# Narrow fp32 products of an attention kernel split into fp32r pairs, with the first image's start reordered and the last store halved

## Reference

```python
# x: (16, 64, 64, 256), W_qkv: (256, 768), W_out: (256, 256), b_out: (256)
g = group_norm(x, 32 groups)                # mean and variance over pixels and 8 channels
q, k, v = split(g @ W_qkv, 3)               # per image: n = 4096 pixels, c = 256 channels
k = softmax(k, over the 4096 pixels)
context = einsum('bdn,ben->bde', k, v)      # 256 x 256 per image
out = einsum('bde,bdn->ben', context, q)
return x + out @ W_out + b_out
```

## Time and profile before

| | |
|---|---|
| median of 3 runs | 1215.73 us (1215.03 to 1215.77) |
| profiled execution | 1216.79 us, of which the span of its instructions 1215.1 us |
| TensorE busy (PE) | 1190.2 us, 98% |
| VectorE (DVE), ScalarE (ACT), GpSimdE (POOL) busy | 840.8, 839.5, 621.4 us |
| HBM traffic | 218 GB/s over the span |

### The profile page before, as it was taken

The page is one execution under the profiler, slowest core; times in us unless marked ns, Lnnn a source line. Parts: engine busy times, 40 slices in busy tenths (PEclk is TensorE's granted clock), DMA queues, the critical chain, the costliest instruction groups (busy, mean ns, idle before and its releaser), DMA issues.

```text
span 1215.1 us, 21446 instructions
## 1 busy us (share of the span) xinstructions
PE 1190.2 (98%) x8460; PEld 1116.2 (92%) x8460; DVE 840.8 (69%) x1582; ACT 839.5 (69%) x1140; POOL 621.4 (51%) x288
## 2 busy tenths in 40 slices
...
GB/s 318 149 166 295 232 234 204 193 273 208 276 200 200 264 172 296 223 206 234 163 302 229 224 220 185 283 208 259 203 206 261 181 281 230 190 254 123 189 84 160
DMA packets 107061, 266.71 MB, mean 219 GB/s; under 512 B 10192, under 2 KB 10192, under 8 KB 106960
## 3 DMA queue, kind: packets, MB, share of 16 engines
...
HBM read 198.18 MB, written 67.11 MB: 218 GB/s over the span
## 4 chain that ended last, share of the span: by engine, by line
PE 96%; DVE 1%; ACT 1%; DMA 1%; issue 0%; SPq 0%; DVEq 0%; ACTq 0%
PE ps_k L385 29%; PE ps_e L548 19%; PE ps_e L557 10%; PE ps_g L476 5%; PE ps_e L464 5%; PE ps_e L476 5%; PE ps_e L466 5%; PE ps_g L464 5%; PE ps_g L466 5%; PE ps_g L495 1%; PE ps_g L512 1%; PE ps_g L526 1%; PE ps_g L518 1%; DVE bn L819 1%; PE ps_g L501 1%; DMA xs<-in_xt_dram 1%
## 5 line engine op out<-in xcount | busy, mean ns | idle before, releaser
L327 POOL TENSOR_TENSOR xt_lo<-xt_raw,xt_hi 128x1024 fp32r<-128x1024 f32 x128 | 307.4, 2404 | 435.3 <-ACT xt_hi L655 309.6
L333 POOL TENSOR_TENSOR x_lo<-x_raw,x_hi 128x1024 fp32r<-128x1024 f32 x128 | 280.2, 2206 | 67.7 <-ACT x_hi L660 58.2
L869 DVE TENSOR_TENSOR mx<-ps_k,mx 128x256 f32<-128x256 f32 x480 | 203.3, 423 | 96.3 <-ACT e_raw L664 74.9
L712 ACT ACTIVATE o_stage<-ps_e,bias 128x512 f32<-128x512 f32 x253 | 170.5, 688 | 114.8 <-PE ps_e L557 114.8
L385 PE MATMUL ps_k<-wk_hi,xt_hi 128*128 128x256 f32 x1024 | 207.3, 285 | 0.0
L385 PE MATMUL ps_k<-wk_lo,xt_hi 128*128 128x256 f32 x1024 | 205.3, 283 | 0.0
L664 ACT ACTIVATE e_raw<-ps_k 128x512 f32<-128x512 f32 x256 | 141.2, 594 | 88.4 <-PE ps_k L385 88.4
L826 DVE BATCH_NORM_STATS2 bn<-xs 128x6 f32<-128x512 f32 x240 | 154.2, 685 | 38.5 <-DMA xs<-in_xt_dram 37.5
L672 ACT ACTIVATE e_hi<-e_raw 128x1024 fp32r<-128x1024 f32 x128 | 135.0, 1055 | 59.1 <-DVE e_raw L894 29.8
L385 PEld LDWEIGHTS ps_k<-wk_hi,xt_hi 128*128 128x128 f32 x1024 | 163.5, 190 | 7.0
L385 PE MATMUL ps_k<-wk_hi,xt_lo 128*128 128x256 f32 x1024 | 158.2, 283 | 0.0
...
## 6 DMA issues: line engine op xcount, KB each, us to landing
xt_raw<-in_xt_dram SPq DMA_DIRECT2D x128, 512.0 KB, 4.3
x_raw<-in_xn_dram SPq DMA_DIRECT2D x128, 512.0 KB, 3.5
out_dram<-o_stage SPq DMA_DIRECT2D x128, 512.0 KB, 4.5
xs<-in_xt_dram SPq DMA_DIRECT2D x240, 256.0 KB, 5.0
w_setup<-in_w_dram SPq DMA_DIRECT2D x2, 256.0 KB, 9.9
wk<-in_w_dram SPq DMA_DIRECT2D x1, 256.0 KB, 10.3
wq_t<-in_w_dram SPq DMA_DIRECT2D x1, 256.0 KB, 11.3
...
```

The costliest lines, as they stand in the source:

```text
L327: nc.gpsimd.tensor_tensor(xt_lo[:, s], xt_raw[:, s], xt_hi[:, s].bitcast(F32), ALU.subtract).then_inc(xt_lo_ready, 1)
L333: nc.gpsimd.tensor_tensor(x_lo[:, s], x_raw[:, s], x_hi[:, s, :, 0:C].bitcast(F32), ALU.subtract).then_inc(x_lo_ready, 1)
L712: nc.scalar.activation(o_stage[:, u % O_SLOTS, h, :], src, ACT.Identity, bias=bias[:, h:h + 1]).then_inc(o_ready, 1)
L869: nc.vector.tensor_tensor(mx[:], tile, mx[:], ALU.max).then_inc(max_done, 1)
```

## The change

The maxima, the variances (from image 1 on) and the negated means are each split on VectorE into an fp32r part and its fp32r rest (new small tiles `m_blk_hi`, `m_blk_lo`, `var_hi`, `var_lo`, `nm_parts`), and the products with them take fp32r operands: 2 matmuls for a plain one in `spread_max` and `stats_var`, and in `bias_sum` the two parts of `m` as weights with both parts of the mean as two columns. `bias_sum` goes from behind the first `emit_high` to behind the second `emit_high` and the first `emit_low`; the bias is added up in two steps. The identity and `grp` are converted to fp32r once, by ScalarE. In image 0 the maxima of block 0 lie in `ps_e`, so that the first gather waits only for `wvo_lo_ready`; half of `wv @ wo` goes behind keys 3; `turn_max` goes behind keys 4 and `spread_max` behind keys 5; shift 3 goes behind the maxima of keys 7, and ScalarE's exponentials 1 and 2 go behind the last `keys_out`. The last chunk is stored in two halves, each when its half is ready.

The diff, cut to its core:

```diff
+        def max_psum(b, blk):
+
+            return ps_e if b == 0 and blk == 0 else (ps_g0, ps_k[:, 0])[blk]
...
+            def store_last():
+                for h in range(CB):
+                    sp.wait_ge(o_ready, B * (CB * NCH) - CB + h + 1)
+                    sp.dma_start(out_chunks[bass.ds((B - 1) * NCH + EMIT_ORDER[NCH - 1], 1), :, h, :].rearrange("a p n -> (a p) n"),
+                                 o_stage[:, (NCH - 1) % O_SLOTS, h, :]).then_inc(last_stored, 16)
...
+                    if b == B - 1 and u == NCH - 1:
+                        store_last()
+                    elif not late(b, u, CB - 1):
                         store(b, u)
...
             def spread_max(b, blk):
 
-                to = (ps_g0, ps_k[:, 0])[blk]
-                pe.wait_ge(m_blk_ready, b * 2 + (blk + 1))
-                for d in range(CB):
-                    last = nc.tensor.matmul(to[:, 1, d * P:(d + 1) * P],
-                                            m_blk[:, blk, d:d + 1].broadcast_to([P, P]), ident,
-                                            start=(d == 0), stop=True, skip_group_check=True)
+                to = max_psum(b, blk)
+                for part, ready in ((m_blk_hi, m_blk_hi_ready), (m_blk_lo, m_blk_lo_ready)):
+                    pe.wait_ge(ready, b * 2 + (blk + 1))
+                    for d in range(CB):
+                        last = nc.tensor.matmul(to[:, 1, d * P:(d + 1) * P],
+                                                part[:, blk, d:d + 1].broadcast_to([P, P]), ident_r,
+                                                start=(part is m_blk_hi and d == 0), stop=(part is m_blk_lo),
+                                                skip_group_check=True)
                 last.then_inc(bc_ps, 1)
...
             def stats_var(b):
-                pe.wait_ge(var2_ready, b + 1)
-                nc.tensor.matmul(stats_psum(b, 1), grp[:], var2[:], start=True, stop=True).then_inc(var_ps, 1)
+                if b == 0:
+                    pe.wait_ge(var2_ready, 1)
+                    nc.tensor.matmul(stats_psum(0, 1), grp_r[:].bitcast(F32), var2[:], start=True,
+                                     stop=True).then_inc(var_ps, 1)
+                    return
+                for part, ready in ((var_hi, var_hi_ready), (var_lo, var_lo_ready)):
+                    pe.wait_ge(ready, b)
+                    last = nc.tensor.matmul(stats_psum(b, 1), grp_r[:], part[:], start=(part is var_hi),
+                                            stop=(part is var_lo))
+                last.then_inc(var_ps, 1)
...
             def gather_high(b, j):
                 pe.wait_ge(e_hi_ready, b * NCH + (j + 1))
-                if j == 0:
+                if b == 0 and j == 0:
+                    pe.wait_ge(wvo_lo_ready, 1)
+                elif j == (HALF if b == 0 else 0):
                     pe.wait_ge(sub_done, b * NCH + HALF)
...
-            def bias_sum(b, parity):
-                pe.wait_ge(m_full_ready, b + 1)
+            def bias_sum(b):
+                pe.wait_ge(nm_parts_ready, b + 1)
+                _, hi, lo = combined(b)
                 for h in range(CB):
-                    for c in range(CB):
-                        last = nc.tensor.matmul(ps_g0[:, 0, h:h + 1], m_full[:, c, h * P:(h + 1) * P],
-                                                neg_mean[:, parity, c:c + 1], start=(h == 0 and c == 0),
-                                                stop=(c == CB - 1), skip_group_check=True)
+                    for part in (hi, lo):
+                        for c in range(CB):
+                            last = nc.tensor.matmul(ps_g0[:, 0, 2 * h:2 * h + 2], part[:, c, h * P:(h + 1) * P],
+                                                    nm_parts[:, c, :], start=(h == 0 and part is hi and c == 0),
+                                                    stop=(part is lo and c == CB - 1), skip_group_check=True)
                 last.then_inc(bias_ps, 1)
...
+            pe.wait_ge(grp_r_ready, 1)
             stats_mean(0)
             stats_var(0)
...
-            for c in range(CB):
+
+            def values_out(c):
                 for e in range(CB):
                     last = nc.tensor.matmul(ps_g0[:, c, 0:C], wv_t[:, e, c * P:(c + 1) * P], wo[:, e, :],
                                             start=(e == 0), stop=(e == CB - 1))
-            last.then_inc(setup_ps, 1)
+                last.then_inc(setup_ps, 1)
+
+            values_out(0)
             first_keys_high()
             keys_low(0, 0, 0, 0, TILES)
             for j in range(1, HALF):
                 keys(0, 0, j)
+            values_out(1)
             pe.wait_ge(wq_loaded, 16)
             for d in range(CB):
-                last = nc.tensor.matmul(ps_e[:, 0, 0:C], one_col[:].broadcast_to([P, P]), wq_t[:, d, :],
+                last = nc.tensor.matmul(ps_e[:, 1, 0:C], one_col[:].broadcast_to([P, P]), wq_t[:, d, :],
                                         start=(d == 0), stop=(d == CB - 1))
             last.then_inc(setup_ps, 1)
-            pe.wait_ge(wvo_lo_ready, 1)
+            keys(0, 0, 4)
+            pe.wait_ge(ident_r_ready, 1)
             turn_max(0, 0)
-            keys(0, 0, 4)
+            keys(0, 0, 5)
+            pe.wait_ge(setup_sb, 2)
             spread_max(0, 0)
-            for j in range(5, NCH):
+            for j in range(6, NCH):
                 keys(0, 0, j)
 
...
                 emit_high(b, parity, 0, 0)
-                bias_sum(b, parity)
+                emit_high(b, parity, 0, 1)
                 emit_low(b, parity, 0, 0)
-                emit_high(b, parity, 0, 1)
+                bias_sum(b)
                 emit_low(b, parity, 0, 1)
...
+            act.wait_ge(consts_ready, 5)
+            nc.scalar.activation(zero_eye_r[:], zero_eye[:], ACT.Copy).then_inc(ident_r_ready, 1)
+            nc.scalar.activation(grp_r[:], grp[:], ACT.Copy).then_inc(grp_r_ready, 1)
...
-            act.wait_ge(consts_ready, 5)
-            act.wait_ge(setup_ps, 1)
-            nc.scalar.activation(wvo_hi[:], ps_g0[:, :, 0:C], ACT.Copy).then_inc(setup_sb, 1)
...
             act.wait_ge(setup_ps, 2)
-            nc.scalar.activation(wq_sum[:], ps_e[:, 0, 0:C], ACT.Copy).then_inc(setup_sb, 1)
+            nc.scalar.activation(wvo_hi[:], ps_g0[:, :, 0:C], ACT.Copy).then_inc(setup_sb, 1)
+            act.wait_ge(setup_ps, 3)
+            nc.scalar.activation(wq_sum[:], ps_e[:, 1, 0:C], ACT.Copy).then_inc(setup_sb, 1)
             nc.scalar.activation(wq_hi[:], wq_t[:], ACT.Copy).then_inc(setup_sb, 1)
             for j in range(4, NCH):
                 keys_out(0, j, 0)
                 keys_out(0, j, 1)
-                if j >= 5:
-                    exps(0, j - 5)
+                if j == 5:
+                    exps(0, 0)
+            exps(0, 1)
+            exps(0, 2)
...
+                dve.wait_ge(var2_ready, b + 1)
+                nc.vector.tensor_copy(var_hi[:], var2[:]).then_inc(var_hi_ready, 1)
+                dve.wait_ge(var_hi_ready, b)
+                nc.vector.tensor_tensor(var_lo[:], var2[:], var_hi[:].bitcast(F32),
+                                        ALU.subtract).then_inc(var_lo_ready, 1)
...
+                dve.wait_ge(m_blk_ready, b * 2 + (blk + 1))
+                nc.vector.tensor_copy(m_blk_hi[:, blk, :], m_blk[:, blk, :]).then_inc(m_blk_hi_ready, 1)
+                dve.wait_ge(m_blk_hi_ready, b * 2 + (blk + 1))
+                nc.vector.tensor_tensor(m_blk_lo[:, blk, :], m_blk[:, blk, :], m_blk_hi[:, blk, :].bitcast(F32),
+                                        ALU.subtract).then_inc(m_blk_lo_ready, 1)
...
+                nc.vector.tensor_copy(nm_parts[:, :, 0], neg_mean[:, parity, :]).then_inc(nm_hi_ready, 1)
+                dve.wait_ge(nm_hi_ready, b + 1)
+                nc.vector.tensor_tensor(nm_parts[:, :, 1], neg_mean[:, parity, :], nm_parts[:, :, 0].bitcast(F32),
+                                        ALU.subtract).then_inc(nm_parts_ready, 1)
...
+                sums = ps_g0[:, 0, 0:2 * CB].rearrange("p (h k) -> p h k", k=2)
+                nc.vector.tensor_tensor(bias_hi[:], sums[:, :, 0], b_mean[:], ALU.add).then_inc(bias_hi_ready, 1)
+                dve.wait_ge(bias_hi_ready, b + 1)
+                nc.vector.tensor_tensor(bias[:], sums[:, :, 1], bias_hi[:], ALU.add).then_inc(bias_ready, 1)
...
-            for q in range(1, 4):
+            for q in range(1, 5):
                 bn_half(1, q)
+            for j in range(HALF):
+                key_maxes(0, j)
+                for q in ((5, 6), (7, 8), (9,), ())[j]:
+                    bn_half(1, q)
             dve.wait_ge(setup_sb, 1)
             nc.vector.tensor_tensor(wvo_lo[:], ps_g0[:, :, 0:C], wvo_hi[:].bitcast(F32),
                                     ALU.subtract).then_inc(wvo_lo_ready, 1)
-            for j in range(HALF):
-                key_maxes(0, j)
-                for q in ((4, 5), (6, 7), (8,), ())[j]:
-                    bn_half(1, q)
+            bn_half(1, 10)
```

(52 more changed lines are left out.)

13 lines of the change are left out of this document (8 added, 5 removed).

## The result

The changed kernel takes 1220.93 us, median of 8 (1219.88 to 1226.26), beside 1215.69, median of 8, of the kernel before: the ratio is 1.0046 (95% interval 1.0035 to 1.0057). It is slower by 0.46%, twice what a measurement tells from no change. The profiled executions are 1219.0 and 1215.1 us long.

The account below looks back on a forecast made before the run. TensorE, busy 98% of the span, was taken to bound the kernel. Products 0, image 0 -1.0, last image +0.9 and last store -0.6 gave -0.7 us, 1215.0 us from 1215.73; own range 1212.8 to 1216.9, with rivals 1212.5 to 1228.5.

Parts of the forecast that it names:

- VectorE's nine operations an image, "0.16 each", at nothing in image 0 with "some 2 us left": VectorE's added two-column operations, some 1.5 us an image, cost nothing; image 0's spreading inputs still have some 2 us left.
- a wait in images 1 to 14: Sign of error: TensorE was to show no wait there, a 24-matmul keys chunk (2.85 us) covering the later bias.
- The split products' price: TensorE's spreading, bias and variance: 286 records before and after, narrow fp32r priced at 0.110 us like plain, so 0 us.
- the faster: Rival: narrow fp32r on TensorE loads weights quicker or hides them, 0.06 us a record, -14 us, 1201; 11%.
- the slower: Rival: TensorE runs a narrow fp32r matmul in several passes, +13 us (1228) or +31 us (1246); 17%, 11% the first.
- Image 0, "-1.0 us": Start of image 0: the second block's transposes start at 51.4 instead of 52.41, after a 1.9 us wait; net -1.0 us.
- the lower of TensorE's two clock levels: Image 0's first keys run at 1.2 GHz, so their 1.1 us head start is worth about 0.6 at 2.4 GHz.
- My range of 1.8 either way around 1215.0: Allowance for TensorE's pace in image 0 rising at 20.4 instead of 24.0, or as much later.
- The last image, "+0.9 us": Later bias leaves the second chunk's emit waiting until 1192.2, TensorE ready at 1191.40: a new stall of 0.9 us.
- The last store, "-0.6 us": End of kernel: with the last chunk in halves only 256 KB remain to store; gain between 0.2 and 0.65, taken as 0.6.
- The sum: Whole kernel: 0 - 1.0 + 0.9 - 0.6 = -0.7 us, so 1215.0 us against the median 1215.73.
- the waits of image 0 go and none comes back: Rival: VectorE's chain in image 0 is shorter by 1.9 us, so the sum is -2.6, 1213.1; no separate chance given.

Follow-up runs that it names:

- e1_plain: The changed kernel with spreading, bias and variance products in plain fp32 again, split tiles and their VectorE operations gone; 1215.48 us, ratio 0.9993 to the kernel before.
- e4_pool_held: The changed kernel with one more wait: in image 0 GpSimd begins its operations for image 1 only when nm_parts is written; 1216.92 us, ratio 1.0010 to before.
- e10_split_all_clear: The changed kernel, its small split operations up to image 1's variance cleared, image 0's reordered, GpSimd held but for an urgent x_lo; 1215.07 us, ratio 0.9988 to before.
- e5_plain_bias_early: e1_plain with the bias back behind the first emit-high half, as in the kernel before; 1215.20 us, ratio 0.9997 to before.
- e2_split_only: The kernel before with the split products alone, image 0 in the old order, the last chunk stored whole; 1219.88 us, ratio 1.0036 to before.

## Why the prediction was wrong, by its steps

**VectorE's nine operations an image, "0.16 each", at nothing in image 0 with "some 2 us left".** This is the step that failed. The four that stand in the second block's chain (with the older `dm`) lasted 0.48, 2.30, 2.25 and 2.17 us; 6.3 us more in a chain with 1 us of idle. Without them, in e1_plain, the stretch is 5.4 us shorter. I took the duration from an operation that reads PSUM (the bias add) and used it for operations from SBUF to SBUF. The trace of before held the sign, and I did not read it. Two groups, of the kernel before and of the kernel after; columns as in the earlier trace rows. Before:

```profile
L886 DVE TENSOR_TENSOR dm<-m_blk,m_all 128x4 f32<-128x4 f32 x16 | 12.2, 766 | 0.5
```

After:

```profile
L948 DVE CAST m_blk_hi<-m_blk 128x2 fp32r<-128x2 f32 x32 | 31.1, 973 | 1.1
L958 DVE TENSOR_TENSOR dm<-m_blk,m_all 128x4 f32<-128x4 f32 x16 | 4.7, 294 | 0.5
```

Four columns at a mean of 766 ns were five times what they compute. After the change the first small operation behind each maximum, `m_blk_hi`, takes that wait over at 973 ns, and `dm` is down to 294. From image 1 on all this lies beside other work and costs nothing, as predicted: TensorE has no wait for these operations there. It does have two for ScalarE's output, 0.25 us at 336.27 and 0.63 at 558.74, and I had said that a wait in images 1 to 14 would show me wrong. They are not shown to be the change's: e4_pool_held and e10_split_all_clear, whose bias stands in the same place in those images, have none, and e5_plain_bias_early, without the split and with the bias in its old place, has one of 0.47 for a GpSimd result.

**The split products' price.** Right: eight bias records take 1194.63 - 1193.82 = 0.81 us, 0.10 each (0.11 predicted); the eight plain ones of e1_plain take 0.81 too (1189.04 to 1189.85). Over images 8 to 12, where neither has a wait that before hasn't, e10_split_all_clear gains 0.09 us an image on before and e1_plain 0.03, so the split itself gives some 0.05 an image, under 1 us in all, where I had 0; which of its products gives it is not shown. Neither rival on this price, the faster and the slower, holds.

**Image 0, "-1.0 us".** Half right. With plain products the transposes start at 51.65 after a wait of 1.6 (51.4 and 1.9 predicted; 52.41 before), and chunk 0's gather is 0.7 ahead. By chunk 7 only 0.1 of that is left, since `e_lo` there lasts 2.78 beside GpSimd: the same mechanism again. I read the slow start of the keys as the lower of TensorE's two clock levels; the granted clock of the profile is 1.00 there (21.5 to 24.0 in the kernel before), so the pace alone speaks for it. The pace rises at a different moment in each execution, at 21.5 us in the earliest of the 13 profiled ones and 25.0 in the latest. My range of 1.8 either way around 1215.0 was for this, and would be 1213.2 to 1216.8, not the 1212.8 to 1216.9 that I wrote.

**The last image, "+0.9 us".** Right: 1195.98 against 1194.63 + 2 x 0.233 = 1195.10, a stall of 0.9; 0.7 with plain products, none with the old place.

**The last store, "-0.6 us".** Right: the span beyond TensorE's last matmul is 0.74 us shorter in every kernel with the halves, 0.0 in e2_split_only.

**The sum.** By the profiled executions the image-0 term is +3.9 in place of -1.0, and the others stand: 3.9 + 0.9 - 0.7, and -0.1 in between, where the cheaper records' 1.2 are nearly used up by two waits for ScalarE's output (0.9 of the L597 row) and small ones. That is 3.9 us; the medians say 5.2. The profiled execution of before ran 1.1 above its median, and that of after started luckily: chunk 0's gather is 2.1 us ahead of before, where the change gives 0.7 (e1_plain, its input complete at 15.86, as late as before's). The other 1.4 are that execution's own, its input complete 0.8 sooner and its pace up at 21.8 instead of 24.0. Without them the image-0 term is 5.9 - 0.7 = +5.2, and the sum 5.3, as the medians have it. The slower side came by a mechanism that none of my rivals named, and "the waits of image 0 go and none comes back" was the reverse of what happened: larger ones came. The step that failed is the first one alone: operations taken at 0.16 us and at nothing, without asking what GpSimd did beside them. That e1_plain, all but the split, is 0.8 below before agrees with my -0.7 partly by luck: the store gives it, not image 0.
